# Embedding tables split in eight pieces, and the next tile's first 13 chunks in one run behind the last logits

## The reference, cut to what matters

```python
seq_embed  = concat([emb_seq[i][seq_inputs[:, :, i]] for i in range(2)])     # 2048 x 40 x 128
item_embed = concat([emb_seq[i][item_inputs[:, i]] for i in range(2)])       # 2048 x 128
q = broadcast(item_embed)
info = concat([q, seq_embed, q - seq_embed, q * seq_embed])                  # 512 wide
h = sigmoid(info @ att_W1 + att_b1)                                          # 80
h = sigmoid(h @ att_W2 + att_b2)                                             # 40
logits = where(seq_inputs[:, :, 0] != 0, h @ att_Wf + att_bf, NEG_INF)
user_info = einsum(softmax(logits), seq_embed)                               # 2048 x 128
x = batchnorm(concat([user_info, item_embed, dense, 3 sparse embeddings]))   # 456 wide
out = sigmoid(prelu(prelu(x @ ffn_W1 + b1) @ ffn_W2 + b2) @ out_W + out_b)
```

## Time and profile before

| what | value |
|---|---|
| median of 3 runs | 1720.0 us (1718.48 to 1723.7) |
| profiled execution | 1716.74 us, its span 1714.2 us |
| TensorE busy | 1460.6 us (85%) |
| VectorE busy | 886.3 us (52%) |
| ScalarE busy | 473.1 us (28%) |
| POOL busy | 1211.3 us (71%) |
| mean granted TensorE clock | 0.927 of full |

### The profile page before, as it was taken

One profiled execution on the slowest core, in us unless ns is written; L12 is line 12 of the kernel. 1 busy time (PEld: TensorE's weight loads), 2 busy tenths in 40 slices (PEclk: granted clock), 3 DMA queues, 4 the chain that ended last, 5 costly groups with the idle time before them and its releaser, 6 DMA issues.

```text
span 1714.2 us, 23508 instructions
## 1 busy us (share of the span) xinstructions
PE 1460.6 (85%) x7609; PEld 799.5 (47%) x7609; DVE 886.3 (52%) x2233; ACT 473.1 (28%) x815; POOL 1211.3 (71%) x1269
## 2 busy tenths in 40 slices
PE   0098997989889897989889897989989898989958
PEld 0055453545455453545445453545545454554522
DVE  3544636454453746455463645445464645546453
ACT  2322223232232313232232313222231313222133
POOL 6877777777777777777767777677767777677700
PEclk9999998989999998999999898999989899998975
DMA  6512112121211212121211212121121112112300
GB/s 123 130 27 45 28 27 46 28 45 27 46 28 27 45 28 46 27 46 27 45 26 27 44 27 46 25 45 25 27 44 28 45 25 45 26 27 45 27 3 0
DMA packets 58900, 64.25 MB, mean 37 GB/s; under 512 B 33351, under 2 KB 33683, under 8 KB 58263
## 3 DMA queue, kind: packets, MB, share of 16 engines
q0 software_dynamic: 40448, 41.50, 14.8%
q1 hardware_dynamic: 17474, 14.55, 3.1%
q10 hardware_dynamic: 850, 6.50, 1.6%
HBM read 62.36 MB, written 0.11 MB: 36 GB/s over the span
## 4 chain that ended last, share of the span: by engine, by line
PE 81%; ACT 8%; DVE 5%; issue 3%; DMA 1%; SPq 1%; ACTq 0%; DVEq 0%
PE grown L427 46%; PE pre L440 8%; PE pre L442 8%; PE mid L449 6%; PE mid L456 5%; PE turned L412 4%; ACT stage L630 2%; ACT hist_t L620 2%; ACT x L595 1%; PE mid L393 1%; ACT L660 1%; DVE sums L922 1%; DVE pre L865 1%; DMA stage<-in_L_rec_emb_seq_dram 1%; SPq L297 1%
## 5 line engine op out<-in xcount | busy, mean ns | idle before, releaser
L337 POOL DMA_INDIRECT hist<-in_L_rec_emb_seq_dram,idx x1184 | 1135.3, 959 | 360.8 <-issue 334.0
L427 PE MATMUL grown<-stage,split 128*128 128x384 bf16 x4704 | 852.7, 334 | 74.2 <-DVE stage L839 74.2
L427 PEld LDWEIGHTS grown<-stage,split 128*128 128x128 bf16 x4704 | 462.3, 100 | 460.4 <-issue 125.1
L839 DVE TENSOR_SCALAR stage<-rel 128x768 bf16<-128x768 bf16 x796 | 384.2, 541 | 0.0
L857 DVE TENSOR_TENSOR prod_t<-turned,item_t 128x512 f32<-128x512 f32 x160 | 110.5, 691 | 403.9 <-ACT hist_t L620 403.9
L625 ACT ACTIVATE hidden<-pre 80x512 f32<-80x512 f32 x160 | 94.6, 592 | 497.7 <-DVE pre L865 497.7
L865 DVE TENSOR_TENSOR pre<-pre,item_part 80x512 f32<-80x512 f32 x160 | 110.8, 693 | 198.3 <-PE pre L442 198.3
L440 PE MATMUL pre<-hist_t,w_hist 128*80 128x512 f32 x320 | 180.0, 646 | 23.6 <-ACT hist_t L620 23.6
L442 PE MATMUL pre<-prod_t,w_raw 128*80 128x512 f32 x320 | 177.3, 638 | 0.0
L922 DVE SCALAR_TENSOR_TENSOR sums<-hist,weight,sums 128x128 f32<-128x128 f32 x576 | 158.1, 348 | 0.0
L449 PE MATMUL mid<-hidden,w 80*64 80x256 f32 x640 | 104.7, 405 | 52.5 <-ACT hidden L625 52.5
(11 more groups left out here) (121 smaller groups left out, 593.0 us busy)
## 6 DMA issues: line engine op xcount, KB each, us to landing
hist<-in_L_rec_emb_seq_dram,idx POOLq DMA_INDIRECT x1184, 2.5
keys<-key_rows SPq DMA_DIRECT2D x34, 384.0 KB, 4.3
stage<-in_L_rec_emb_seq_dram ACTq DMA_DIRECT2D x4, 1372.0 KB
sparse_rows<-in_L_rec_emb_sparse_dram,idx_sparse POOLq DMA_INDIRECT x48, 3.3
stage<-in_L_rec_emb_seq_dram ACTq DMA_DIRECT2D x4, 183.8 KB
raw<-in_r_seq_inputs_dram SPq DMA_DIRECT2D x1, 600.0 KB, 17.3
items<-in_L_rec_emb_seq_dram,idx POOLq DMA_INDIRECT x32, 3.5
w_raw<-in_L_rec_att_W_dram SPq DMA_DIRECT2D x1, 160.0 KB
```

Source lines behind the costliest of these rows:

```text
L337: gp.indirect_dma_start(rows, None, table, bass.IndirectOffsetOnAxis(ap=index, axis=0)).then_inc(landed, 16)
L427: last = nc.tensor.matmul(grown[n][:, 0:MC], split[n][:, c, k, :], hot[:, slot, n * MC:(n + 1) * MC], start=(c == 0 and k == 0), stop=(c = ...
L839: last = nc.vector.tensor_scalar(hot[:, slot, :], rel[half][:, :, 0:RC], float(c), None, ALU.is_equal)
```

## The change

The tables go through in eight pieces. `stage` is gone; `hot` and the small tiles have a buffer of their own (`pool`), and the pieces land in three slots (`SLOTS`) in the second half of `hist`, which the gathers of tile 1 fill later. A piece is a range of chunks of one table (`RANGES`: 13, 12, 12, 12 chunks with both halves), and even and odd table rows now sit side by side in place of lower and upper half, so the key is row >> 1 and the choice row & 1. ScalarE and VectorE work on piece after piece; TensorE waits for them range by range. Keys are computed from the sequence indices alone, which SP loads ahead of the weights; ScalarE's queue loads them back in the middle of the splitting, and the first 13 one-hots are made between pieces. TensorE does tile 0's first 13 chunks before the loop. In a tile each early group has five chunks, one more stands behind group 6, and 13 of the next tile stand behind the last logits (after tile 15 too, into a tile that isn't used). Group 7 is transposed with the early groups; `turn_rows` writes into `turned`. On VectorE `add_item(EARLY)` and `pick` stand ahead of the early weights' sums, and the next tile's one-hots lie in pairs between the sums.

```diff
-    PER = 6
+    PER = 5
+    AHEAD = 13
+    RANGES = [(0, 13), (13, 25), (25, 37), (37, 49)]
+    PIECES = len(RANGES) * NB
+    SLOTS = 3
-        stage = sb("stage", [P, 2, CH * E])
-        pool = stage.rearrange("p s e -> p (s e)")
+        pool = sb("pool", [P, spare + N // 2 + 3 * D])
+        staged = [hist[:, 1, k * PIECE:(k + 1) * PIECE].rearrange("p (c e) -> p c e", e=2 * E) for k in range(SLOTS)]
...
@@ SP: sequence indices ahead of the weights, items' and sparse indices last; keys 0 and 1 no longer here
+                sp.dma_start(raw[:, 1:TILES, 0:SEQ], seq_t[:, 1:TILES, :]).then_inc(seq_rest_loaded, 16)
                 sp.dma_start(w1_raw[:, :, :], att_w1.rearrange("(c p) n -> p c n", p=P)).then_inc(att_weights_loaded, 16)
...
@@ POOL
                     wait(gp, tile_consumed, tile + 2)
+                    if half == 1:
+                        wait(gp, piece_ready, PIECES)
...
@@ TensorE
-            pe.wait_ge(piece_ready, 2 * NB)
+            def grow(tile, half, first, end):
+                for c in range(first, end):
+                    slot = (half * CH + c) % HOTS
+                    for r, (begin, _) in enumerate(RANGES):
+                        if c == begin:
+                            pe.wait_ge(piece_ready, NB * (r + 1))
+                    pe.wait_ge(hot_ready, tile * CH + (c + 1))
+                    ...
+            grow(0, 0, 0, AHEAD)
             with pe.Fori(0, PAIRS) as pair:
...
-                    pe.wait_ge(rows_copied, tile + 1)
-                    grow(0, PER)
...
                     for g in range(EARLY):
-                        if g + 1 < EARLY:
-                            turn_group(g + 1)
-                        grow(g * PER + 6, g * PER + 8)
+                        at = AHEAD + g * PER
+                        turn_group(g + 1)
+                        grow(tile, half, at, at + 2)
                         layer1(g)
-                        grow(g * PER + 8, g * PER + 10)
+                        grow(tile, half, at + 2, at + 4)
...
-                        grow(g * PER + 10, g * PER + 12)
+                        grow(tile, half, at + 4, at + PER)
+                    grow(tile, half, CH - 1, CH)
                     logits_of(EARLY - 2)
                     layer2(EARLY - 1)
                     logits_of(EARLY - 1).then_inc(early_logits_done, 1)
-                    turn_group(EARLY)
-                    grow((EARLY + 1) * PER, CH)
                     layer1(EARLY)
+                    turn_group(EARLY + 1)
                     pe.wait_ge(softmax_step, tile * 4 + 3)
                     layer2(EARLY)
+                    pe.wait_ge(picked_ready, tile + 1)
+                    layer1(EARLY + 1)
                     logits_of(EARLY)
-                    turn_group(EARLY + 1)
-                    layer1(EARLY + 1)
                     turn_group(EARLY + 2)
+                    layer2(EARLY + 1)
                     layer1(EARLY + 2)
+                    logits_of(EARLY + 1)
                     turn_rows()
-                    layer2(EARLY + 1)
-                    logits_of(EARLY + 1)
                     layer2(EARLY + 2)
                     logits_of(EARLY + 2).then_inc(logits_done, 1)
+                    grow(tile + 1, 1 - half, 0, AHEAD)
...
@@ ScalarE, head (split_high and split_middle are the casts; load_piece three DMAs)
+            def split_middle(q):
+                act.wait_ge(rest_ready, q + 1)
+                ...
+                if q + SLOTS < PIECES:
+                    act.wait_ge(piece_ready, q + 1)
+                    load_piece(q + SLOTS)
+            for q in range(SLOTS):
+                load_piece(q)
+            for q in range(PIECES):
+                split_high(q)
+                if q > 0:
+                    split_middle(q - 1)
+                if q == 3:
+                    ...
+                if q == 4:
+                    act.wait_ge(keys_stored, 16)
+                    load_keys(0, 0)
+                    load_keys(1, 1)
+                if q == 5:
+                    act.wait_ge(lanes_ready, 1)
+                    act.wait_ge(keys_landed[0], 32)
+                    relate(0).then_inc(rel_ready, 1)
+            split_middle(PIECES - 1)
@@ ScalarE, loop
                     sigmoid2(EARLY - 3)
+                    copy_group(EARLY, EARLY % 2)
                     sigmoid1(EARLY - 1, 0)
                     sigmoid2(EARLY - 2)
                     sigmoid2(EARLY - 1)
-                    copy_group(EARLY, EARLY % 2)
...
@@ VectorE, head (before: all four pieces, then scales, indices, then 12 one-hots)
+            rest(0)
+            rest(1)
+            low(0)
             dve.wait_ge(att_weights_loaded, ATT_LOADS)
...
+            for q in range(2, PIECES):
+                rest(q)
+                low(q - 1)
+                if q == 6:
+                    dve.wait_ge(rel_ready, 1)
+                    heat(0, 0, 0, AHEAD)
+            low(PIECES - 1)
@@ VectorE, behind the early logits
-                    product(EARLY, EARLY % 2)
+                    add_item(EARLY, EARLY % 2)
+                    pick()
+                    dve.wait_ge(rel_ready, tile + 2)
+                    heat(tile + 1, 1 - half, 0, 2)
                     wait(dve, early_weights_ready, tile + 1)
                     add_group(0, begin=("empty", "empty"))
+                    product(EARLY + 1, (EARLY + 1) % 2)
                     add_group(1)
-                    add_item(EARLY, EARLY % 2)
+                    heat(tile + 1, 1 - half, 2, 4)
+                    add_item(EARLY + 1, (EARLY + 1) % 2)
                     add_group(2)
-                    pick()
+                    heat(tile + 1, 1 - half, 4, 6)
+                    product(EARLY + 2, (EARLY + 2) % 2)
                     add_group(3)
+                    heat(tile + 1, 1 - half, 6, 8)
+                    add_item(EARLY + 2, (EARLY + 2) % 2)
                     add_group(4)
+                    heat(tile + 1, 1 - half, 8, 10)
...
+                    heat(tile + 1, 1 - half, 10, AHEAD)
```

More of the change, by code:

```diff
@@ L419, in turn_group @@
                         last.then_inc(group_turned, 1)
[L421 to L430, removed]
                     def turn_rows():
                         for j in range(MP):
-                            last = nc.tensor.transpose(grown[0][:, j * P:(j + 1) * P], hist_t[:, LAST % 2, (j + 1) * P:(j + 2) * P],
+                            last = nc.tensor.transpose(turned[0][:, j * P:(j + 1) * P], hist_t[:, LAST % 2, (j + 1) * P:(j + 2) * P],
                                                        ident[:, :])
@@ L711, in _ @@
             dve.sem_inc(rel_used, 1)
-            for slot in range(2):
-                last = nc.vector.memset(stage[3 * P // 4:P, slot, SHORT * E:CH * E], 0.0)
-            last.then_inc(stage_cleared, 1)
+            for k in range(SLOTS):
+                last = nc.vector.memset(staged[k][3 * P // 4:P, :, :], 0.0)
+            last.then_inc(table_cleared, 1)
             nc.vector.memset(w2[:, :], 0.0)
@@ L722, in _ @@
                 nc.vector.memset(x[h][:, :, :], 0.0)
+            nc.vector.memset(user[:, :], 0.0)
             dve.sem_inc(softmax_step, 2)
@@ L748, in _, with rest, low, heat @@
             row_numbers(0, 0)
+            def rest(q):
+                n, (first, end), k = q % NB, RANGES[q // NB], q % SLOTS
+                dve.wait_ge(high_ready, q + 1)
+                whole = staged[k][:, 0:end - first, :]
+                nc.vector.tensor_tensor(whole, whole, split[n][:, first:end, 0, :], ALU.subtract).then_inc(rest_ready, 1)
+            def low(q):
+                n, (first, end), k = q % NB, RANGES[q // NB], q % SLOTS
+                dve.wait_ge(middle_ready, q + 1)
+                nc.vector.tensor_tensor(split[n][:, first:end, 2, :], staged[k][:, 0:end - first, :], split[n][:, first:end, 1, :],
+                                        ALU.subtract).then_inc(piece_ready, 1)
+            def heat(tile, half, first, end):
+                for c in range(first, end):
+                    slot = (half * CH + c) % HOTS
+                    dve.wait_ge(hot_used, tile * CH + (c + 1))
+                    last = nc.vector.tensor_scalar(hot[:, slot, :], rel[half][:, :, 0:RC], float(c), None, ALU.is_equal)
+                    last.then_inc(hot_ready, 1)
+                if end == CH:
+                    dve.wait_ge(hot_ready, tile * CH + CH)
+                    dve.sem_inc(rel_used, 1)
+            rest(0)
+            rest(1)
+            low(0)
             dve.wait_ge(att_weights_loaded, ATT_LOADS)
@@ L833, in _ @@
             nc.vector.tensor_copy(dense_now[:, 0, :], dense_rows[:, 0, :]).then_inc(dense_ready, 1)
-            def heat(tile, half, first, end):
-                for c in range(first, end):
-                    slot = (half * CH + c) % HOTS
-                    dve.wait_ge(hot_used, tile * CH + (c + 1))
```

(7 more changed lines are left out.)

150 lines of the change are left out of this document (67 added, 83 removed).

## The result

The changed kernel takes 1705.8 us (median of 4 runs, 1704.0 to 1706.5) against 1719.2 for the kernel before on the same chip (1716.8 to 1723.7): ratio 0.992, 95% interval 0.990 to 0.994. It is faster by 13.4 us, where 31 had been forecast; the time lies at the upper edge of the forecast's own range, 1672 to 1706. The profiled execution has a span of 1704.5 us at a mean granted clock of 0.935 (before 1714.2 and 0.927).

A forecast was written before the change was run, and what follows sets the result against it. TensorE's own time and idle time were taken as the bound. 78.5 + 15 x 97.06 + 81.2 + 15.8 + 51.8 = 1683.2 us of span, 31 less; so 1689 measured, own range 1672 to 1706, chance 0.38.

The forecast's parts named there:

- Head: Before tile 0's item transposes: eight pieces through three slots bring these to 78.5 us, a gain of 13, bounds 3 and 20.
- Rival B: Head gains little: ScalarE's in-order queue becomes the bound, tile 0 starts at 88, time 1698 us; chance 0.17.
- Chunks moved: In each tile's groups: moving chunks into the run costs nothing; without VectorE's cover, up to 0.98 us a group.
- Late part: Behind group 6's logits: gain 1.2 us a tile at equal clock, bounds -2.5 and +2.6.
- Rival C: The late part is no shorter, VectorE being its bound: 18 us less gain, 1707 us; chance 0.18.
- Clock: TensorE's loss to lower clock in late part and run stays as today: zero, bounds plus 3.4, minus 4.6 us a tile.
- Loop's jump: At every second tile's end: TensorE's own jump back, 3.09 us of idle, now following 12.7 us of dense work.
- end: After the last logits: an unused run of 12.7 us plus the loop's end 3.1, so 15.8 instead of 8.2.
- A: The clock stays up in and after the sparse part: about 1654 us; chance 0.17.
- D: Slower: drops on every tile's run and after odd tiles' loop gap (3.4 us each), VectorE costs 1; 1742 us, chance 0.10.
- tile 15: The last tile, without its six and one chunks and with the late part's 1.2: 81.2 us, not 88.8.
- POOL's tile: POOL issues 76 gathers a tile, one every 1.24 us, about 94.5 us: no tile can come faster for long.

The follow-up runs named there:

- e3: The changed kernel with VectorE making one-hots 13 to 17 ahead of products 0 and 1, not behind them: 1669.7 us, ratio 0.974.
- e4: The changed kernel with one-hots 13 to 17 ahead of products 0 and 1, and 18 to 20 ahead of product 2: 1627.4 us, ratio 0.950.
- e7: The changed kernel with only one-hots 18 to 20 moved ahead of product 2: 1656.3 us, ratio 0.967.
- e5: The kernel before, with VectorE making six one-hots ahead instead of twelve, so none stay in hand: 1750.6 us, ratio 1.020.
- e9: The changed kernel, VectorE's order untouched, TensorE running 8 chunks instead of 13 behind the logits and before the loop: 1655.2 us, ratio 0.968.
- e6: e4 with TensorE's run of 13 chunks moved behind the loop's jump, none for tile 16: 1624.6 us, ratio 0.946.
- e10: e4 with the run of 13 behind the loop's jump and group 7's addition behind two weighted sums: 1646.5 us, ratio 0.961.
- e8: e4 with VectorE's addition for group 7 put back behind two weighted sums: 1626.9 us, ratio 0.949.

## Why the prediction was right or wrong

The sign was right and the size was not: 13 us in place of 31. My own sign of being wrong, a mean tile of 98 or more, has come (98.97). By the prediction's own steps:

- **Head** (forecast 78.5, measured 73.95): right in mechanism. The relation was computed at 52.8, where I had 55 and more, and the one-hots began at 58.4; the first fetch issued at 6.2. The attention weights were usable at 22.5, so the 600 KB of indices ahead of them did no harm; SP's queue stood at one issue for 9.40 us where it had stood for 13.05; what held it, no run separates. Rival B is out.
- **Chunks moved, "VectorE has some 4 us in it, so I cost this at nothing"**: this is the step that failed. I had added up VectorE's work in a group and not asked in which order it comes. The run of 13 uses every one-hot that was made ahead; before, six of twelve were left when a tile began. The two waits that this opens are 66.6 / 16 = 4.2 us a tile, and some 72 us with what follows from them (e3, e4, e7); e5 and e9 show that the spare one-hots are what decides. The bound that I wrote beside it, "each group could wait up to the 0.98 us that it lost", was a bound on work and not on order, and it was exceeded: two groups lose 1.9 to 2.8 us each.
- **Late part** (forecast gain 1.2, measured 21.7 - 1.4 - 17.1 = 3.2): better than forecast. The hand count of 16.3 us at full clock is what e4 takes in half of its tiles. What was off is the clock: I added its loss to the 16.3, giving 19, while it costs 0.8 to 1.1 us (17.1 in the changed kernel, 17.4 in e4's other tiles), not 2.7. The lower level stretches matmuls into time in which they would have waited: the waits of 0.80 and 0.25 us that e4's tile 7 has ahead of layer 2 of group 8 and layer 1 of group 9 are gone in tile 7 of the changed kernel, and the 1.37 ahead of the last layer 2 is 0.69. Rival C is out, though its 1707 is the nearest number: the tile gained in the late part and lost more in the groups.
- **Clock** (forecast zero): about right outside the late part as a sum and wrong in its places. The run of 78 has full clock in all 16 tiles (12.84 us), where the 36 before lost 1.8 on average; in the tile behind the jump the two twelves lose 1.8 and 1.7 us instead. The second comes behind a one-hot stall and goes with it in e4, the first stays there (4.05 us at 824.86). The Trainium skill (TensorE: Matmul & The Clock Gate, HAM oscillation) advises to put contraction steps in one row so that the clock stays up. The trace agrees for the changed kernel, and e4 and e6 go against it as a general rule: there the same row of 78 starts low and takes 14.5 to 15.7 us in about half of the tiles.
- **Loop's jump**: I left its 3.1 us as they were. In the changed kernel TensorE is idle for 1.04 us at that place, with the run of 78 ahead of the jump; in e6 with no run ahead of it it is 3.10 again. That the jump passes while the 78 still run is my reading of these two, not measured by itself. A second idle time follows, 0.74 us ahead of the transposes at 866.38, to which the profile gives no releaser; each of the seven jumps has one, of 0.5 to 1.0 us. At the **end** no idle time of the jump shows, 12.7 us and not 15.8.
- **Rivals A and D**: both speak of the clock. A (1654), that it stays up, is not what e4 shows at 1627: there the waits are gone and most tiles still have a drop. Of D's two drops the one on the run did not come, but the one behind the loop gap did, in every second tile, 1.8 of its 3.4 us by itself; the other 1.7 came with the wait before chunk 18. e10 shows a third pair, late part and run, and what it costs.
- **Luck**: the miss of 17 us is the rest of two larger ones that work against each other. e4, which has no waits, takes 94.0 us a tile where 97.06 was forecast: late part 16.9 for 19.0, run 13.6 for 14.6, jump 0.5 for 1.5, and the groups 63.1 for 61.8 (the 67.2 of before without six chunks and with group 7's transposes). The changed kernel is 5.0 us a tile above that. The forecast was some 3 us a tile too dark in what it counted and left out 5.
- **Sums**: tile 15 was put at 81.2, but 88.8 less seven chunks (6.8) and 1.2 is 80.8; measured were 83.0. The 94.5 us of POOL's tile are 94.2 by 76 x 1.24, and 94.9 in the trace of e4.

A tile, from 98.26: late part -3.2, clock on the first chunks -1.8, jump -1.0 (half of 3.1 - 1.0), one-hot waits +4.2, clock on the twelves +1.7 (3.4 in every second tile) give 98.2; 98.97 was measured. Most of the 0.8 us between them lies behind the jump: from the item transposes to chunk 13 TensorE takes 5.43 us in tile 8 (863.50 to 868.93, with the second idle time in it) and 4.16 in tile 7 (766.70 to 770.86), 0.6 a tile on the mean.

## What to carry to other kernels

Where one engine makes small pieces ahead for another, count how many are left in hand at each point of the cycle, and not only whether the maker has time on average: a move that uses up the stock turns the maker's place in its own order into a wait. Then put those pieces ahead of the maker's next blocking wait; here two such moves were worth some 72 us and the large change 13. And a stall with a clock drop behind it is only worth removing for the drop's sake if no other place takes the drop over: here two changes of stalls that cost nothing alone cost 22 us together, so test them in pairs.

## What the runs showed of the hardware that I had not expected

- In the late part and the run behind it the lower clock acts as one drop that moves. With the stall ahead of layer 2 at 1.08 us it fell on the following run of matmuls in 7 tiles and inside the part in 8 (e4), with 2.65 us always inside the part (e8); part and run together were the same within 0.3 us in the tiles shown, and the kernels within 0.5 us. Two long idle times around one late part (2.66 at 808.16 and 3.30 at 824.20 in e10) brought two. What puts a drop here or there is not shown.
- A row of 78 matmuls with no wait in it does not keep the clock up: it took 12.84 us, or 14.5 to 15.7 (e4, e6), with 0.60 and 0.54 of the clock granted in its first 4 us (e4, 806 to 810).
- A loop's jump leaves TensorE idle for 3.0 to 3.6 us with no run of matmuls ahead of it (before, e6, e10), and for 0.7 to 1.3 us with 78 ahead of it (863.50 after, 821.26 in e4), then for 0.5 to 1.0 us more three microseconds later. In the changed kernel the profile puts the first of these down to VectorE's copy behind its own jump (L911), in e4 at 821.26 to nothing.
- Half clock does not double a stretch in which TensorE partly waits: 0.8 to 1.1 us on 16.3.
